# 672 table gathers written out in two kinds of pass of a four-layer graph network, with their indices read in place

## What is computed

```python
# L0, in each of T = 3 rounds: the score of each edge
x_i = x[dst]
x_j = x[src] + edge_attr
q = (x_i @ wq.T + bq).reshape(-1, HEADS, DH)
k = (x_j @ wk.T + bk).reshape(-1, HEADS, DH)
alpha = jnp.sum(q * k, axis=-1) / jnp.sqrt(jnp.float32(DH))
...
# L3, once
score = K[src] * Q[dst] / np.sqrt(DH)
s = jnp.exp(jnp.clip(jnp.sum(score, axis=-1), -5.0, 5.0))
wV = jax.ops.segment_sum(V[src] * s[..., None], dst, num_segments=n)
z = jax.ops.segment_sum(s[..., None], dst, num_segments=n)
```

## Time and profile before

| what | us |
|---|---|
| device time, median of three runs | 12465.03 |
| lowest and highest of the runs | 12452.8, 12473.96 |
| the profiled execution, first to last instruction (its span) | 12433.7 |
| POOL busy in the span | 6378.4 |
| gathers of the three score passes, busy | 2045.3 |
| gathers of the transformer pass, busy | 675.5 |

### The profile page before, as it was taken

How to read it: one execution, slowest core, us unless ns; L and a number is a source line. 1 busy time by engine, 2 the same in 40 slices (tenths; PEclk the granted TensorE clock), 3 DMA queues, 4 the chain that set the end, 5 groups by cost and what they waited for, 6 DMA issues and landing times. The chain is left out here.

```text
span 12433.7 us, 154586 instructions
## 1 busy us (share of the span) xinstructions
PE 6625.2 (53%) x36192; PEld 5643.9 (45%) x36193; DVE 4969.4 (40%) x11746; ACT 2217.8 (18%) x4249; POOL 6378.4 (51%) x6364
## 2 busy tenths in 40 slices
PE   4555687555687555686334333533533343355555
PEld 3555674555574555674333232333323333334443
DVE  4444664444674444673223221322312232235555
ACT  1222453222453222452000000000000000011111
POOL 2555432555432555431664566366366636625553
PEclk6777898777798777797556665655755575577777
DMA  2333321333331333330111211111111111112221
GB/s 78 112 113 114 101 85 51 113 111 113 97 90 47 113 113 115 99 89 20 45 45 32 72 45 45 57 45 45 53 50 45 44 59 45 45 39 78 77 77 56
DMA packets 698397, 893.93 MB, mean 72 GB/s; under 512 B 148418, under 2 KB 443212, under 8 KB 698131
## 3 DMA queue, kind: packets, MB, share of 16 engines
q0 software_dynamic: 198368, 429.61, 13.5%
q1 hardware_dynamic: 498474, 461.96, 11.8%
q10 hardware_dynamic: 1416, 0.86, 0.0%
HBM read 698.72 MB, written 193.14 MB: 72 GB/s over the span
## 5 line engine op out<-in xcount | busy, mean ns | idle before, releaser
L851 POOL DMA_INDIRECT l_sums_ring<-table_typed,tile_idx x2512 | 2482.8, 988 | 1773.3 <-issue 727.3
L960 PE MATMUL psum<-l_sums_ring,select 128*128 x7840 | 1669.2, 393 | 3039.8 <-DVE acc L941 1086.8
L821 POOL DMA_INDIRECT acc<-table_x,index x2016 | 2045.3, 1015 | 2166.5 <-DVE index L816 1541.0
L960 PEld LDWEIGHTS psum<-l_sums_ring,select 128*128 128x128 f32 x7840 | 1513.3, 293 | 3198.5 <-issue 3195.3
L941 DVE TENSOR_TENSOR acc<-acc,psum 128x128 f32 x980 | 280.5, 286 | 3179.6 <-remote 2414.8
L1078 PE MATMUL psum<-ident,select 128*128 128x128 f32 x2016 | 435.4, 355 | 1493.1 <-ACT l_scores_mixT L1018 507.6
L1053 DVE TENSOR_TENSOR acc<-l_scores_key,psum 128x512 f32<-128x512 f32 x504 | 345.9, 686 | 1776.8 <-ACT l_scores_key L1026 1331.8
L1078 PEld LDWEIGHTS psum<-ident,select 128*128 128x128 f32 x2016 | 295.5, 180 | 1569.1 <-issue 947.7
L821 POOL DMA_INDIRECT l_pass_ring<-table_kv,index x672 | 675.5, 1005 | 635.5 <-issue 264.4
L851 POOL DMA_INDIRECT l_sums_ring<-table_x,tile_idx x628 | 618.2, 984 | 634.6 <-ACTq L78 335.0
L925 DVE SCALAR_TENSOR_TENSOR select<-dst_all,pair_start,iota_row 128x512 f32<-128x512 f32 x980 | 732.5, 748 | 524.8 <-issue 407.9
(11 more groups left out here) (343 smaller groups left out, 10753.4 us busy)
## 6 DMA issues: line engine op xcount, KB each, us to landing
acc<-in_edge_attr_dram SPq DMA_DIRECT2D x2016, 64.0 KB
rows_dram<-l_scores_mixT SPq DMA_DIRECT2D x504, 256.0 KB
l_values_ring<-rows_dram SPq DMA_DIRECT2D x504, 256.0 KB
table_typed<-l_rows_rows SPq DMA_DIRECT2D x40, 1024.0 KB, 4.3
l_sums_ring<-table_typed,tile_idx POOLq DMA_INDIRECT x2512
acc<-table_x,index POOLq DMA_INDIRECT x2016
l_pass_ring<-table_kv,index POOLq DMA_INDIRECT x672
table_x<-l_rows_rows SPq DMA_DIRECT2D x40, 256.0 KB, 2.3
```

Source lines behind the costliest of these rows:

```text
L821: pool.indirect_dma_start(out=ring[:, at, u, :], out_offset=None, in_=table, in_offset=bass.IndirectOffsetOnAxis(ap=index[:, at % REGIONS, ...
L851: pool.indirect_dma_start(out=ring[:, k % TILE_RING, u, :], out_offset=None, in_=table, in_offset=at).then_inc(gathered[k % REGIONS], 16)
L960: ins = pe.matmul(sums(k), select[:, k, u, :], rows, start=u == 0, stop=u == GROUP - 1)
```

## The change

All 168 regions are written out in both kinds of pass, as a plain loop of the program text, with the index column a constant place in `src_idx`. POOL itself waits until the region four back is free: in the score pass until it is turned (`p_turned`), in the transformer pass until it is weighted (`p_weighted`). The copies of indices, their tile and their semaphore are gone; with them DVE's `ask`.

```diff
-        index = sb("index", [P, REGIONS, GROUP], I32)
...
-        def copy_index(dve, i, r):
-            dve.tensor_copy(index[:, r, :], src_idx[:, bass.ds(step_of(i, r), GROUP)]).then_inc(p_index, 1)
-
-        def gather(pool, ring, table, at):
-            for u in range(GROUP):
-                pool.indirect_dma_start(out=ring[:, at, u, :], out_offset=None, in_=table,
-                                        in_offset=bass.IndirectOffsetOnAxis(ap=index[:, at % REGIONS, u:u + 1], axis=0)
-                                        ).then_inc(gathered[at % REGIONS], 16)
-
-        def gathers(pool, ring, table, used=None):
-            def body(i):
-                for r in range(REGIONS):
-                    pool.wait_ge(p_index, region_of(i, r) + 1)
-                    if used:
-                        at_least(pool, used, region_of(i, r) - (REGIONS - 1))
-                    pool.sem_inc(gather_go, 1)
-                    gather(pool, ring, table, r)
-            turns(pool, body)
+        def gathers_by_step(pool, ring, table, freed):
+            for k in range(STEPS // GROUP):
+                if k >= REGIONS:
+                    pool.wait_ge(freed, k - REGIONS + 1)
+                    pool.sem_inc(gather_go, 1)
+                for u in range(GROUP):
+                    at = bass.IndirectOffsetOnAxis(ap=src_idx[:, k * GROUP + u:k * GROUP + u + 1], axis=0)
+                    pool.indirect_dma_start(out=ring[:, k % REGIONS, u, :], out_offset=None, in_=table, in_offset=at
+                                            ).then_inc(gathered[k % REGIONS], 16)
...
-                        gathers(pool, ring, table_x[:])
+                        gathers_by_step(pool, ring, table_x[:], p_turned)
...
-                        def ask(i, r):
-                            dve.wait_ge(p_turned, region_of(i, r) + 1)
-                            if nxt := led(i, r, REGIONS):
-                                copy_index(dve, *nxt)
-
                         def body(i):
                             for r in range(REGIONS):
-                                ask(i, r)
                                 if nxt := led(i, r):
                                     lead(*nxt)
...
-                        for r in range(REGIONS):
-                            copy_index(dve, 0, r)
                         lead(0, 0)
...
-                        gathers(pool, ring, table_kv[:], p_weighted)
+                        gathers_by_step(pool, ring, table_kv[:], p_weighted)
...
-                                if later := led(i, r, REGIONS):
-                                    copy_index(dve, *later)
...
-                        for r in range(REGIONS):
-                            copy_index(dve, 0, r)
```

More of the change, by code:

```diff
@@ L800, in _ @@
                             sp.wait_ge(stored, 16 * (CHUNKS // V))
-        p_index, p_selected, p_mixed, p_turned, p_spread, p_projected = sems(
-            "index_copied", "selected", "mixed", "edges_turned", "turned_copied", "projected")
+        p_selected, p_mixed, p_turned, p_spread, p_projected = sems(
+            "selected", "mixed", "edges_turned", "turned_copied", "projected")
         p_evacuated, p_multiplied, p_scored, p_score_kept = sems("evacuated", "multiplied", "scored", "score_kept")
@@ L982, in queries @@
                     return psum[:, 4 + 2 * (r % 2):6 + 2 * (r % 2), 0:pair * Q_W].rearrange("p a (b w) -> p a b w", w=Q_W)
-                with block(name, p_index, p_selected, p_mixed, p_turned, p_spread, p_projected, p_evacuated, p_multiplied, p_scored,
+                with block(name, p_selected, p_mixed, p_turned, p_spread, p_projected, p_evacuated, p_multiplied, p_scored,
                            p_score_kept, *p_in, *p_out) as b:
@@ L1240, in sums @@
                     return psum[:, 4 + 2 * (r % 2) + u // 2, (u % 2) * W:(u % 2 + 1) * W]
-                with block(name, p_index, p_selected, p_turned, p_spread, p_projected, p_multiplied, p_evacuated, p_scored,
+                with block(name, p_selected, p_turned, p_spread, p_projected, p_multiplied, p_evacuated, p_scored,
                            p_weight, p_weighted, p_summed, p_added) as b:
```

## The result

The changed kernel takes 12130.26 us (median of 4, 12114.06 to 12145.02) against 12463.52 of the kernel before on the same chip: a ratio of 0.973 [0.972, 0.974], 333 us less where 61 were forecast. The profiled execution has a span of 12136.3 us.

The account below looks back on a forecast made before the run. The prediction saw no engine full and a loop of waits, held in the score passes by PE's late results. Terms of 40 + 7 + 10 + 4 = 61 us, taken from 12465, gave 12404 us; range 12130 to 12530.

Parts of the forecast that it names:

- term 3: Score passes: POOL waits for the turned region itself and may run ahead; 10 us saved, bounds 0 and 544.
- the lead pays: Score passes: POOL's 5.4 us idle is on the loop after all, pace moves towards the sum pass's; 12142 us, chance 0.15.
- slower: Score passes: POOL's pause let PE's results through; without it they are held longer; 12607 us, chance 0.20.
- Term 1: Score passes: DVE loses 504 index copies, counted where PE waits for the mix; 40 us saved, bounds 0 and 106.
- Term 2: Transformer pass: DVE loses 168 index copies, nearly free there; 7 us saved, bounds 0 and 13.
- Term 4: Starts of passes: first gathers start earlier, but the transformer's is slowed beside DVE's clearing; 4 us saved, bounds 0 and 8.
- Term 5: Written-out code: 672 gathers in the program instead of 16 in a loop; cost 0.
- The prediction's own sign of being wrong: A score pass shorter by over 50 us (lead on the loop), or longer with more "remote" time before ACT's copies.

Follow-up runs that it names:

- late event run: Changed kernel, but in the score passes GpSimd also waits until VectorE has kept the previous region's score; 12429.58 us, ratio 0.998 in a held job.
- e9: Changed kernel, but in the score passes VectorE mixes into the attributes' buffer, so GpSimd waits for that mix, not TensorE; 12545.67 us, ratio 1.0064.
- copies kept: Changed kernel, but VectorE still makes all 672 index copies at their old places, unused by GpSimd; 12137.56 us, ratio 0.9734 in a held job.
- e7: The held run of the copies kept: changed kernel with VectorE's unused index copies at their old places; 12137.56 us, ratio 0.9734.
- e11: Changed kernel, but score-pass gathers wait until TensorE has turned the region after the one they replace; 12032.22 us, ratio 0.9713.
- e4: The held late event run: changed kernel, GpSimd also waiting for VectorE's kept score of the previous region; 12429.58 us, ratio 0.998.
- e5: Changed kernel, but in the score passes GpSimd waits before each region's gathers until the region before has landed; 12627.08 us, ratio 1.0141.
- e10: Changed kernel, but score-pass gathers wait until VectorE has kept the score of the region they replace; 12469.21 us, ratio 1.0004.
- m1: Control: changed kernel with two sum-pass waits taking the larger of count and 1, in a prompt job; 10623.77 us, ratio 1.0004.
- m2: Control: changed kernel with two sum-pass waits taking the larger of count and 1, in a held job; 12031.27 us, ratio 0.9716.

## Why the prediction was wrong

**The step that failed is term 3, GpSimd's lead**, taken as 10 us with 0 and 544 as bounds. By the late event run it is about 310. I chose the end near 0 since "nothing but 46.4 us waited for gathers". That row was read rightly and is still true (41.8 us after). What was wrong is the step from it: that an engine on which nobody waits can't be on the loop. The loop's link was not the rows that GpSimd fetches but the time in which it fetches them, since in a held job many of TensorE's results are seen only once a run of gathers is over. The rows that said so stood in the prediction: 310.7 us of "remote" at ACT, and keys 2.9 us after the last gather's start. It named TensorE's late results as what holds the loop, and used them for two rivals, but not for term 3.

**The rival "the lead pays"**, 12142 at 0.15, came true within 12 us, its reason in brackets included. The number was half of a bound, so its closeness is luck.

**The rival "slower"** had the mechanism and the wrong sign. It took it that GpSimd, knowing of a free region at 658.21, would go on without a pause. It mostly can't: its new wait is itself for a result of TensorE, and in after the runs end after 4 or 8 gathers, before that result is seen. So the pause stays, and ends with the result, after 2 us and not 5. Where GpSimd's wait is freed of TensorE (e9) the time did go up, to 12546, on the side of the rival's 12607; but its pauses got longer there, 355 us a pass, and not rarer, so that is no proof of its sum.

**Term 1**, 40 us for 504 copies: too high. 6 to 22 by the copies kept, at most 25 with the written-out code by the late event run. Its lower bound of 0 had the late results as its reason; no run shows whether they are why it came out low. **Term 2**, 7 us: the transformer pass didn't get shorter, 1151 us against 1145. There GpSimd still waits for VectorE's weighted message, 176.6 us before and now

```profile
POOL l_pass_ring L820 <- DVE score L1276: 277.6, 88, 7.5
```
**Term 4**: the first gather ran beside the clearing and took 6.36 us where 6.62 was forecast. It ended at 10882.65, 1.09 us behind the clearing's end, so starting early gave next to nothing, as the row of the sum pass said. The Trainium skill, page "SBUF — State Buffer", section "SBUF: two separate sides", states such a blocking for VectorE's two-port modes; it doesn't say of this chip that a clearing is one, as the prediction took it, and the 6.36 us are the trace's own evidence that this one blocks. **Term 5**, 0: right within the 25 us that the late event run leaves for copies and code together. The range, 12130 to 12530, just held the 12130.26.

The prediction's own sign of being wrong, a score pass shorter by over 50 us ("then the lead was on the loop"), is what the after trace shows, and the late event run bears it out.

## What to carry to other kernels

An engine that no one waits for can still set the pace, if its activity delays others' results: look at what the late releases coincide with (here, often the end of a run of gathers), not only at who waits for its data. Where results come through mostly in an engine's pauses, let that engine's pause end with the first such result, and not with work that stands behind several; a buffer freed earlier by another engine can cost (e9, 1.0064). And compare a kernel with itself over several jobs before reading a gain: this one is 2.7 and 2.8% in two held measurements and nil in a prompt one.

## What was unexpected of the hardware

- The same program took 10622 and 12382 us in two jobs with the same chip number. From first to last gather a score pass took 857 against 1030 us (m1 and m2). What differs between the jobs was not found.
- In held jobs TensorE's results can reach the other engines late (17.8 us in the unit shown) while GpSimd issues gathers back to back, and in time when it pauses for 2.4 us after every four. No run here shows where the delay arises. The Trainium skill, page "SBUF — State Buffer", section "SBUF: two separate sides", says that TensorE and ScalarE never wait for another engine at its ports; so by the page it doesn't arise at those ports, and no run here tests that.
- A held job loses time in every pass with gathers, not in the score passes alone: from first to last gather the five sum passes took 4566 us in m2 and 3993 in m1, the transformer pass 1147 and 860. Pauses there were not tried. Of the held kernels that do all the work none beats the change: e7 and e11 equal it, e4, e5, e9 and e10 lose.
